# A fused attention and FFN block: masked weights corrected on 64x64 blocks, rotations one slot later

## The reference

```
q = xn @ Wq -> 32 heads of 64;  k, v = xn @ Wk, xn @ Wv -> 8 heads of 64;  rope on q and k
allowed = (j <= i) & (i - j < 128)                 # a causal window of 128 keys
attn = softmax(where(allowed, q k^T / 8, -inf));   out = (attn @ v) @ Wo
ffn: x = fwht(xn * SU) / 64;  h = silu(gate) * up;  fwht(h * SU2) / 64 @ W_down, with scales
```

## Time and profile before

| | us |
|---|---|
| median of 3 runs (1433.56 to 1437.24) | 1434.48 |
| the profiled execution's own time | 1436.66 |
| its span, first to last instruction | 1434.6 |
| TensorE busy | 1340.1 (93%) |
| VectorE / ScalarE / GpSimd busy | 900.7 / 753.2 / 677.1 |
| granted TensorE clock, mean | 0.986 of 2.4 GHz |

### The profile page before, as it was taken

How to read it: one execution, slowest core, us unless ns; L and a number is a source line. 1 busy time by engine, 2 the same in 40 slices (tenths; PEclk the granted TensorE clock), 3 DMA queues, 4 the chain that set the end, 5 groups by cost and what they waited for, 6 DMA issues and landing times. The chain is left out here.

```text
span 1434.6 us, 34061 instructions
## 1 busy us (share of the span) xinstructions
PE 1340.1 (93%) x12776; PEld 1045.3 (73%) x12776; DVE 900.7 (63%) x1496; ACT 753.2 (53%) x2685; POOL 677.1 (47%) x719
## 2 busy tenths in 40 slices
PE   6889888999999999999999999999999999999998
PEld 3676666867778677877778677786777877787776
DVE  6657664467755677457773677546775477745775
ACT  2355654266643666346662666536664466634665
POOL 5225533065532665336651565416654266523664
PEclk9899989999999999999999999999999999999999
DMA  6223341423423342323424244143332234231342
GB/s 229 70 59 119 108 140 52 118 75 104 119 66 84 107 115 86 105 62 97 124 62 133 55 112 124 37 118 89 92 117 85 78 100 116 82 110 46 90 112 60
DMA packets 71554, 138.35 MB, mean 96 GB/s; under 512 B 15328, under 2 KB 29152, under 8 KB 71136
## 3 DMA queue, kind: packets, MB, share of 16 engines
q1 hardware_dynamic: 70400, 135.46, 32.6%
q10 hardware_dynamic: 992, 0.73, 0.2%
HBM read 73.21 MB, written 12.58 MB: 60 GB/s over the span
## 5 line engine op out<-in xcount | busy, mean ns | idle before, releaser
L485 POOL TENSOR_TENSOR e_sb<-e_sb,rinv 128x512 f32<-128x512 f32 x256 | 266.6, 1042 | 367.8 <-DVE rinv L830 360.3
L592 ACT ACTIVATE e_sb<-S,negmax 128x128 f32<-128x128 f32 x1024 | 363.0, 369 | 110.0 <-DVE negmax L825 108.9
L602 ACT ACTIVATE pt_sb<-TR 128x512 f32<-128x512 f32 x256 | 153.2, 599 | 174.8 <-PE TR L1048 173.9
L818 DVE COPY_PREDICATED S<-diagonal_key,S 128x512 f32<-128x512 int8 x192 | 133.1, 693 | 171.8 <-PE S L1037 169.5
L709 DVE TENSOR_TENSOR prod<-PROJ,rope_sb 128x1024 f32<-128x1024 f32 x160 | 195.0, 1219 | 64.3 <-PE PROJ L895 63.4
L1037 PEld LDWEIGHTS S<-k_stack,q_stack 64*64 64x64 f32 x5632 | 172.1, 133 | 74.7 <-issue 49.5
L1048 PE MATMUL TR<-ident,e_sb 128*128 128x128 f32 x1024 | 168.8, 288 | 55.8 <-POOL e_sb L485 49.7
L1037 PE MATMUL S<-k_stack,q_stack 64*64 64x64 f32 (+2 forms) x5632 | 214.1, 276 | 0.0
L592 ACT ACTIVATION_READ_ACCUMULATOR e_sb<-S,negmax 128x1 f32 x1024 | 211.8, 207 | 0.0
L825 DVE TENSOR_REDUCE negmax<-S 128x4 f32<-128x512 f32 x256 | 176.9, 691 | 8.8
L1048 PEld LDWEIGHTS TR<-ident,e_sb 128*128 128x128 f32 x1024 | 108.6, 141 | 88.0 <-POOL e_sb L485 73.1
(11 more groups left out here) (96 smaller groups left out, 2659.8 us busy)
## 6 DMA issues: line engine op xcount, KB each, us to landing
q_stack<-qy SPq DMA_DIRECT2D x512, 64.0 KB, 2.0
wq_ring<-wq_split_d SPq DMA_DIRECT2D x56, 512.0 KB, 3.8
wo_ring<-wo_split_d SPq DMA_DIRECT2D x56, 512.0 KB, 3.9
k_stack<-ky SPq DMA_DIRECT2D x256, 64.0 KB, 3.0
x_in<-x SPq DMA_DIRECT2D x8, 512.0 KB, 4.5
wq_split_d<-wq_ring SPq DMA_DIRECT2D x8, 512.0 KB, 3.7
wo_split_d<-wo_ring SPq DMA_DIRECT2D x8, 512.0 KB, 4.3
out<-acc SPq DMA_DIRECT2D x8, 512.0 KB, 4.9
```

What stands on the lines that cost most here:

```text
L485: nc.gpsimd.tensor_tensor(e, e, r, ALU.mult).then_inc(norm_done, 1)
L592: last = nc.scalar.activation(e_sb[:, n % 2, r, :], s_heads(n, 1)[:, r, :], ACT.Exp, bias=negmax[:, n % 2, r:r + 1], accum_out=rowsum[:, n ...
L602: nc.scalar.activation(pt_sb[:, n % 4, :, :], TR[:, :, :], ACT.Copy).then_inc(t_copied, 1)
```

## The change

**Values.** The square is taken apart at 64. Queries 0 to 63 (half a = 0) and 64 to 127 (a = 1) are multiplied separately, in two PSUM banks: half 0 in O, half 1 in the first half of the TR bank. The first product takes pt_sb unmasked with v[i-1] for the queries of half 0, and for half 1 with a new tile **v_mix** that holds v[i] for keys 0 to 63 and v[i-1] for keys 64 to 127. What is left to correct is one 64x64 block for each half: 64 keys, 64 queries, four such products in a step with i > 0 and none in a step with i = 0. `mask` is left out for steps with i = 0. `values_mixed` takes two steps at once: first all products of pt_sb, then all corrections. O is evacuated in two operations on ScalarE and two on VectorE in place of one each.

**Waits.** `values_mixed` waits for the copy of the transposes of step n-2, since it writes into their bank; transposes of odd slots wait for o_low, for the same reason.

**Order.** In odd slots TensorE does the transposes behind the fillers, no longer ahead of them. VectorE takes `inverse_sum` and `o_low` to the head of odd slots, ahead of `fold`. GpSimd rotates one slot after the job's second part and ahead of `mask`. The job table puts both parts of a job into even slots; row_normalised writes a tile of its own, xn, one slot later. SyncE loads and saves Wq blocks at other places of its list.

```diff
-    ROPE_SLOTS = {("q", 2, 0): (0, 1), ("q", 3, 0): (4, 5), ("q", 4, 0): (7, 8), ("k", 1, 0): (10, 11),
...
+    ROPE_SLOTS = {("q", 2, 0): (0, 1), ("q", 3, 0): (4, 5), ("q", 4, 0): (6, 8), ("k", 1, 0): (10, 12),
...
-    NORM_SLOT = 24
...
+    NORM_SLOT = 25
...
-    WQ_SPLIT_SLOT = {5: 4, 9: 5, 12: 6, 18: 7}
+    WQ_SPLIT_SLOT = {4: 4, 9: 5, 12: 6, 20: 7}
...
+        O_half = [O[:, 0:2 * P].rearrange("p (s m q) -> p s m q", s=2, m=2),
+                  TR[:, 0:2, :].rearrange("p s (m q) -> p s m q", m=2)]
...
+                    m = {2: 5, 3: 6, 5: 7}.get(n)
+                    if m:
+                        if not b:
+                            save_wq(m - 2)
+                        load_wq(b, m)
...
-                for n in range(STEPS + 2):
+                for n in range(LAST_SLOT + 2):
                     if 1 <= n <= STEPS:
                         normalise(n - 1)
-                    if n >= 2:
+                    for kind, m, row in rope_jobs(b, n - 1, 1):
+                        rotate(row, kind, m)
+                    if 2 <= n <= STEPS + 1 and (n - 2) % TT:
                         mask(n - 2)
...
+                    for a in range(2):
+                        last = nc.scalar.activation(o_half(0, i, a), O_half[a].rearrange("p s m q -> p m s q"), ACT.Copy)
+                    last.then_inc(o_copied, 1)
...
+                def value_mix(i):
+
+                    dve.wait_ge(v_done, b * TT + i + 1)
+                    HP = P // 2
+                    nc.vector.tensor_copy(v_mix[0:HP, i - 1, :], v_sb[0:HP, i, :])
+                    nc.vector.tensor_copy(v_mix[HP:P, i - 1, :], v_sb[HP:P, i - 1, :]).then_inc(v_mixed, 1)
+
                 for n in range(LAST_SLOT + 1):
-                    if n < STEPS:
-                        fold(n)
-                    if 1 <= n <= STEPS:
+                    if 1 <= n <= STEPS and n % 2:
                         inverse_sum(n - 1)
                     if n >= 5 and n % 2:
                         o_low(b, (n - 5) // 2)
+                    if n < STEPS:
+                        fold(n)
+                    if 1 <= n <= STEPS and n % 2 == 0:
+                        inverse_sum(n - 1)
+                    if n in (0, 3, 4):
+                        value_mix(max(n - 1, 1))
...
+                    if n >= 3 and n % 2:
+
+                        pe.wait_ge(o_split, (b * STEPS + n - 3) // 2 + 1)
...
+                def values_mixed(pair):
+
+                    HP = P // 2
+                    pe.wait_ge(t_copied, b * STEPS + min(2 * pair + 3, STEPS))
...
+                    for s in range(2):
+                        g, i = divmod(2 * pair + s, TT)
+                        heads = slice(g * D, (g + 1) * D)
+                        for a in range(2):
+                            v = v_mix[:, i - 1, heads] if i and a else v_sb[:, max(i - 1, 0), heads]
+                            for odd in range(2):
+                                last = nc.tensor.matmul(O_half[a][odd * D:(odd + 1) * D, s, :, :], v,
+                                                        pt_sb[:, (2 * pair + s) % 4, odd:REP:2, a * HP:(a + 1) * HP],
+                                                        start=s == 0, stop=False)
...
+                            for odd in range(2):
+                                for a in range(2):
+                                    half = slice(a * HP, (a + 1) * HP)
+                                    last = nc.tensor.matmul(O_half[a][odd * D:(odd + 1) * D, s, :, :],
+                                                            v_step[half, i - 1, heads], p_cur[half, (2 * pair + s) % 4, odd:REP:2, half],
+                                                            start=False, stop=s == 1)
...
-                    if 2 <= n <= STEPS + 1:
+                    if 2 <= n <= STEPS + 1 and n % 2 == 0:
                         transposes(n - 2)
...
+                    if 2 <= n <= STEPS + 1 and n % 2:
+                        transposes(n - 2)
```

More of the change, by code:

```diff
@@ L123, in place, with masks_upto @@
         return TURN[what] % 2, TURN[what] + 1
+    def masks_upto(n):
+        return n - n // TT
+    MASKS = masks_upto(STEPS - 1)
     def stacked(b, g, semaphores, each):
@@ L402, in _ @@
                         save_wo(1)
[L403 to L408, removed]
                     if n >= 3:
@@ L412, in _ @@
                         load_wo(b, n - 1)
+                    m = {2: 5, 3: 6, 5: 7}.get(n)
[3 more added lines that the diff above has]
+                        load_wq(b, m)
+                    if n >= 6:
+                        if not b:
+                            save_wq(n)
+                        if b + 1 < BATCH:
+                            load_wq(b + 1, n - 6)
                 if not b:
@@ L516, in _ @@
                         value_step(max(n - 1, 1))
-                    for kind, m, row in rope_jobs(b, n, 1):
-                        rotate(row, kind, m)
         @block.scalar
@@ L1049, in transposes @@
                     last.then_inc(t_ready, 1)
[L1051 to L1070 removed]
+                def values_mixed(pair):
+                    HP = P // 2
+                    pe.wait_ge(t_copied, b * STEPS + min(2 * pair + 3, STEPS))
+                    pe.wait_ge(v_done, b * TT + min(2 * pair + 2, TT))
+                    pe.wait_ge(v_mixed, b * (TT - 1) + min(2 * pair + 1, TT - 1))
+                    if pair:
+                        pe.wait_ge(o_split, b * STEPS // 2 + pair)
+                    for s in range(2):
[7 more added lines that the diff above has]
+                                                        start=s == 0, stop=False)
+                    pe.wait_ge(v_stepped, b * (TT - 1) + min(2 * pair + 1, TT - 1))
+                    for s in range(2):
+                        g, i = divmod(2 * pair + s, TT)
+                        heads = slice(g * D, (g + 1) * D)
+                        if i:
+                            pe.wait_ge(p_masked, b * MASKS + masks_upto(2 * pair + s))
+                            for odd in range(2):
+                                for a in range(2):
+                                    half = slice(a * HP, (a + 1) * HP)
+                                    last = nc.tensor.matmul(O_half[a][odd * D:(odd + 1) * D, s, :, :],
+                                                            v_step[half, i - 1, heads], p_cur[half, (2 * pair + s) % 4, odd:REP:2, half],
+                                                            start=False, stop=s == 1)
+                    last.then_inc(pv_done, 2)
```

42 lines of the change are left out of this document (12 added, 30 removed).

## The result

The changed kernel takes **1457.78 us** (median of 4 runs, 1457.7 to 1459.81). The kernel before took 1435.86 in the same runs (1433.56 to 1438.25). The ratio is 1.0156, with a 95% interval of 1.0138 to 1.0174: slower by 22 us, where I had forecast 29.5 less. The range of 1382 to 1430 does not hold it, and rival C, the one on this side, is not what happened either: the copies of O behave as I had costed them.

A forecast was written before the change was run, and what follows sets the result against it. TensorE, busy 93% of the span, was taken as the bound. Six inner rows at -3.4, row 0 at -7.4 and row 7 at -1.7 gave -29.5 off a span of 1434.6: forecast 1405 us, range 1382 to 1430.

The forecast's parts named there:

- rival C: Evacuation of O: each piece costs what the whole did, 73 us more, 1478 in all; chance 0.08.
- -2.8 - 2.0 + 0.6 = -4.2 for the values: Per row: -2.8 from smaller corrections, -2.0 from no pause behind them, +0.6 from values waiting for the transposes' copy.
- +0.9 + 2.2 - 3.0 + 0.8 - 0.1 = +0.8 for order and rotation together: Per row: early slots +0.9, late q_stack +2.2, e_sb waits behind slot 7 gone -3.0, xn +0.8, tail -0.1.
- The waits that I walked: Slots 2 to 7: transposes wait 2.0 in step 2 (0.7 before), 1.95 in slot 7 (0.9 before); +0.9 a row.
- a granted clock that falls within rows 1 to 7: Last of the listed signs that would show the forecast wrong; no size or chance given.
- the -0.63: Two pairs of value steps: corrections save 0.07 in one and 0.28 in the other, plus 0.14 of pause behind each.
- The wait of values for their copy, the +0.6: Shared bank: values wait some 0.14 in every second pair for the copy of the transposes; bounds 0 and +4.8 a row.
- the -4 for the splits: Row 0: VectorE's waits for ScalarE's weight splits, 24.3 us before, change by -4, some now holding up o_low about 2 us.
- +2.5: Row 7, even slots 26 to 32 without projection: the copy wait stands bare, +2.5 over four pairs.
- the 0.8 of xn: Slots 25 and 26: row_normalised ahead of wo_add delays values, about 1.4 over a common slot for 0.6; +0.8 a row.
- the copy loop: From the end of O through transposes, exps and t_copy to the next values: 5.48 us, against TensorE's 5.5 or 5.3.
- rotation and stack: Late rotations of jobs 5 to 7 and their DMAs take 14.6 to 15.3; scores wait 1.1 twice a row, +2.2.

The follow-up runs named there:

- rot: The changed kernel with GpSimd's rotations moved back to the slot of the job's second part, behind the mask: 1420.86 us, ratio 0.9906.
- old_values_rot: The changed kernel with both the values (128x128 corrections, one bank) and the rotations of the kernel before: 1418.34 us, ratio 0.9874.
- warm: The changed kernel with matmuls nobody reads, filling TensorE's idle time ahead of the transposes of slots 4 and 7: 1444.1 us, ratio 1.0063.
- rot_first: The changed kernel with only the rotations of q jobs 2 and 3 moved back, the others late: 1426.98 us, ratio 0.9935.
- old_values: The changed kernel, late rotation included, with values multiplied as before (one bank, no v_mix, no transposes waiting for o_low): 1443.6 us, ratio 1.006.

## Why the prediction was wrong

rot and old_values_rot cut the change in three: the order (old_values_rot against before), the values (rot against it), and the late rotation (the changed kernel against rot). Attention, in us, from windows of the profiled executions; for rows 1 to 6 the mean:

| | rows 1 to 6, each | row 0 | row 7 |
|---|---|---|---|
| order | -2.8 | -0.3 | -2.1 |
| values | -0.6 | +2.7 | +2.7 |
| late rotation | +6.4 | -0.5 | +5.0 |
| sum | +3.0 | +1.9 | +5.6 |
| forecast | -3.4 | -7.4 | -1.7 |

6 x 2.96 + 1.9 + 5.6 = 25.3; row 0 begins 1.1 earlier and the FFN stages give 1.1, which leaves the 23.1 between the spans. In an inner row the forecast had -2.8 - 2.0 + 0.6 = -4.2 for the values, and +0.9 + 2.2 - 3.0 + 0.8 - 0.1 = +0.8 for order and rotation together. Measured are -0.6 and +3.6. Two steps failed: the values were mis-sized (3.6 a row), and the clock stood at nothing (most of 2.8 a row).

**Order and rotation, +3.6 for +0.8.** The waits that I walked are there at their size: 1.9 to 2.1 in slot 4 of rows 1 to 7 (forecast 2.0), 1.8 to 2.24 in slot 7 (1.95). For q_stack slots 20 and 24 idle 0.36 to 1.99, 1.0 in the mean of rows 1 to 6 (1.1). What failed is the last line of the prediction: "a granted clock that falls within rows 1 to 7" stood there as a sign that would prove me wrong, with no price and no chance. I had doubled two waits to 2 us each and gone on adding in microseconds at full clock. The 10 stretches in rows 1 to 6, each 3.4 us at half clock, cost up to 1.7 each, 2.8 a row at the most. By warm it is 13.7 us for 11 of them (1.25 each, 2.1 a row), and 2.4 a row between the lengths of rows 1 to 6. So the clock is most of the 2.8 that is missing; 0.4 to 0.7 of it is not placed.

**Values, -0.6 for -4.2.** The arithmetic was right: two pairs of slots with the old values took 14.68 (690.87 to 705.55, slots 20 to 23 in old_values_rot) and two pairs of the changed kernel that do not wait for q_stack (slots 12 to 15) 6.91 + 7.14 = 14.05, which is the -0.63 that the prediction had for two pairs. What failed was to take that for every pair of the row. It holds for common slots only, and not at three others:
- The *tail* had -0.1 and takes +1.2. In slot 32 transposes stand directly behind those of slot 31, in the one bank, and the values behind both. The 0.78 stands in old_values_rot too, the 1.27 is new:

```profile
753.24 0.63 PE L1080 MATMUL TR<-ident,e_sb 128*128 128x128 f32 x4 [0.78 <-ACT pt_sb L621]
...
756.54 0.44 PE L1097 MATMUL O<-pt_sb,v_sb 128*64 128x128 f32 x4 [1.27 <-ACT pt_sb L621]
```

- The *start* had its share of the -0.63 and takes +0.2. A value_mix is dearer than my bounds (0.2 to 1.3 for its two copies): 0.51 + 0.92 in the mean, of which the group of the second copy shows:

```profile
L886 DVE COPY v_mix<-v_sb 64x512 f32<-64x512 f32 x24 | 22.0, 916 | 0.3
```

- The *x slot*: its values idle 0.41 and the transposes of slot 27 another 0.2, which they don't with the old values. In rot slots 10, 14, 18 and 22 also idle 0.1 to 0.3 for e_sb.

**The wait of transposes for transposes.** In even slots they wait 0.13 or 0.34 for t_copy of those at the end of the odd slot, the pause of 0.09 included (0.18 of it at 664.58 above, by the ends). Old and new values have it alike, so it is in the order's -2.8; my walk had left it out, and it makes the pairs 6.91 and 7.14 for the forecast's 6.75 and 7.04. The wait of values for their copy, the +0.6, did not come: in slots 6 to 24 of row 3 of the changed kernel no values wait.

**Rows 0 and 7.** In row 0 the values take 2.7 more, where the forecast had its -4.2, and order and rotation together 0.8 less, where it had 3.2 less with the -4 for the splits. The waits of the changed kernel's row 0:

```profile
DVE wo_ring L683 <- ACT wo_ring L569: 16.1, 5, 4.6
DVE wq_ring L686 <- ACT wq_ring L564: 13.2, 4, 6.8
```

Together 29.3, for 24.3 and 8.1 for Wq before: 3 less. But they now hold up o_low, and TensorE's transposes wait 19.6 us for it in this row, 8 times. I had named that cost and set it too low; how the 19.6 divide between values and order was not taken apart.

In row 7 the values cost 2.7, where the forecast had -4.2 + 2.5 = -1.7. In its even slots from 26 on, which have no projection, the values do wait for the copy, as here in rot:

```profile
1389.17 0.44 PE L1097 MATMUL O<-pt_sb,v_sb 128*64 128x128 f32 x4 [1.16 <-ACT pt_sb L621]
```

That makes slots 24 to 30 of row 7 1.9 longer than with the old values; the tail adds 1.3, and slots 8 to 23 give back only 0.6. The sum of the prediction also had a slip here: its -1.7 counts the savings of the four pairs (some 0.3 each) beside the +2.5, which was worked out against the old times and holds them already. The rest of row 7 is order and rotation, -2.1 + 5.0, where the forecast had +0.8 less the 0.8 of xn and nothing for the clock.

**What was right.** The evacuation: pieces of O take 0.38 on ScalarE and 0.40 to 0.41 on VectorE (forecast 0.40 and 0.68 for two, measured 0.64 from 662.30 to 662.94), and from slot 9 on no transposes of an inner row wait for o_low. (Two chains were added up a little wrong: the printed terms of the copy loop give 5.45 for 5.48, those of rotation and stack 14.4 to 15.1 for 14.6 to 15.3. Neither changes what failed.) The pause of 0.09 into 64x64 tiles and none out of them, as the Trainium skill has it (TensorEngine Tiling (Array Packing), Key Properties); by the same page's Instruction Overhead the added matmuls would have cost 13 us, an estimate, and the trace does not show it (0.22 for half the columns of 0.43). The agreement of rot's 123.2 with my 123.3 for an inner row is chance: it has no late rotation, and its values brought less.

What stays open: of the 30.8 us of jobs 2 and 3, some 14 are the clock (warm). The remaining 17 have the size of the two waits less the 1.7 that rot idles in slots 3 to 5 (2.06 + 2.24 - 1.7 = 2.6, in seven rows 18), but were not taken apart.

## What to carry to other kernels

Moving an operation one slot later on an engine with time to spare is not free by that alone: follow its single buffers (here prod) and everything that stands behind the next writer, up to the engine that bounds the kernel. On TensorE price an idle stretch of 2 us higher than its length, since the clock may fall behind it, and try a change in its parts: here the order alone was worth more than all three parts together, and the part with the arithmetic nothing. Look at first rows and last slots by themselves; the largest gain of this study, 25 us, lay in row 0, in VectorE's waits for the weight splits, which the change had not been about.

## What the hardware showed that I had not expected

**The clock.** TensorE's granted clock falls to half for 3.4 us in a kernel in which it is busy 91% of the time: behind 10 of the 14 waits of 1.8 to 2.24 us in slots 4 and 7 of rows 1 to 7, and once behind a wait of 2.0 for q_stack. It does not fall behind the other four, nor in rows 1 to 6 of rot and rot_first, whose longest waits are 1.3 and 1.7 us. So the length of a wait alone does not settle it: of the seven waits of 2.2 to 2.4 in slot 4 of old_values it fell behind three. Matmuls without use in the idle stretch keep it (warm).

**Copies beside GpSimd.** The same copy of a 64x512 tile on VectorE takes 0.42 with GpSimd idle, and 1.17 beside its `normalise`, which itself takes 1.22 for 1.04. Slots 1 to 4 of row 1 of the changed kernel, all engines:

```profile
291.80 0.42 DVE L886 COPY v_mix<-v_sb 64x512 f32<-64x512 f32 x1
...
301.13 1.22 POOL L504 TENSOR_TENSOR e_sb<-e_sb,rinv 128x512 f32<-128x512 f32 x1
301.47 1.17 DVE L886 COPY v_mix<-v_sb 64x512 f32<-64x512 f32 x1
```

The pair is much the same in the other rows: 0.83 for the first value_mix, which is what I had put (0.9), and 1.7 for the other two in rows 1 to 7 (1.6 to 1.95), where GpSimd works. That `normalise` is the one the transposes of slot 4 wait for. No run took the copies alone away, so what they cost in all is not shown.
